# Two transformer layers on one core: the second half's route, its scatter, the weight units and the norm moved to other places in the queues

## What is computed

```python
# layer 0: attention by a running sum, then a mixture of experts
kvt = jnp.cumsum(k * v, axis=-2) * denom
vhat = q * kvt
scores = jax.nn.sigmoid(xf @ gate_w.T)
topk_w, topk_idx = jax.lax.top_k(scores, TOP_K)          # 2 of 8 experts
topk_w = topk_w / (topk_w.sum(axis=-1, keepdims=True) + 1e-20)
shared_out = jax.nn.silu(xf @ shared_wg.T) * (xf @ shared_wu.T) @ shared_wd.T
h = jax.nn.silu(jnp.einsum('td,efd->etf', xf, exp_wg)) * jnp.einsum('td,efd->etf', xf, exp_wu)
all_out = jnp.einsum('etf,edf->etd', h, exp_wd)
```

## Time and profile before

| | us |
|---|---|
| median of 3 runs | 780.81 (777.93 to 781.98) |
| profiled execution | 781.96 |
| its span, first to last instruction | 780.1 |
| PE busy in the span | 678.9 (87%) |
| DVE busy | 523.9 (67%) |
| ACT busy | 390.6 (50%) |
| POOL busy | 355.2 (46%) |

### The profile page before, as it was taken

How to read it: one execution, slowest core, us unless ns; L and a number is a source line. 1 busy time by engine, 2 the same in 40 slices (tenths; PEclk the granted TensorE clock), 3 DMA queues, 4 the chain that set the end, 5 groups by cost and what they waited for, 6 DMA issues and landing times.

```text
span 780.1 us, 13300 instructions
## 1 busy us (share of the span) xinstructions
PE 678.9 (87%) x4656; PEld 543.7 (70%) x4656; DVE 523.9 (67%) x1004; ACT 390.6 (50%) x679; POOL 355.2 (46%) x299
## 2 busy tenths in 40 slices
PE   5897898894959879799989989989988998999996
PEld 4675677784848667577667767767866777777774
DVE  6885855884886746567485858486768668467745
ACT  3644423442543644274575455385448276447263
POOL 1416276376576226145163527164616353416353
PEclk9999899897998999999999999999999999999999
DMA  8427735766885274512003303002402000201100
GB/s 313 130 94 223 267 121 179 224 202 221 294 277 181 77 279 116 179 25 58 2 2 108 82 2 82 2 1 69 121 2 65 19 1 28 62 23 44 39 2 28
DMA packets 66804, 82.76 MB, mean 106 GB/s; under 512 B 7090, under 2 KB 50354, under 8 KB 66738
## 3 DMA queue, kind: packets, MB, share of 16 engines
q1 hardware_dynamic: 63156, 73.39, 29.7%
q0 software_dynamic: 3072, 8.39, 3.3%
q10 hardware_dynamic: 512, 0.13, 0.1%
HBM read 40.34 MB, written 28.84 MB: 89 GB/s over the span
## 4 chain that ended last, share of the span: by engine, by line
PE 37%; ACT 9%; DVE 9%; issue 5%; DMA 2%; POOL 2%; ACTq 1%; POOLq 0%; DVEq 0%
PE acc L632 4%; PE acc L634 3%; PE acc L633 3%; PE pv L632 2%; PE pm L632 2%; PE pm L634 2%; PE pm L633 2%; PE pv L634 2%; PE pv L633 2%; PE ring L955 2%; PE ring L985 2%; DVE hf L2067 2%; DVE mx L2151 2%; ACT act L1428 1%; PE ring L957 1%
## 5 line engine op out<-in xcount | busy, mean ns | idle before, releaser
L1531 POOL TENSOR_TENSOR hl<-hf,hh 128x512 fp32r<-128x512 f32 (+1 forms) x76 | 99.3, 1307 | 231.5 <-ACT hh L1235 231.4
L1235 ACT ACTIVATE hh<-hf 128x512 fp32r<-128x512 f32 (+1 forms) x76 | 47.7, 629 | 85.5 <-DVE hf L2067 69.8
L632 PE MATMUL acc<-hh,wh 128*128 128x512 f32 (+1 forms) x168 | 70.6, 420 | 7.6 <-POOL hl L1531 7.6
L2067 DVE TENSOR_TENSOR hf<-hf,pv 128x512 f32<-128x512 f32 x64 | 43.6, 682 | 39.7 <-PE pv L634 38.6
L2151 DVE TENSOR_REDUCE mx<-ring 128x2 f32<-128x512 f32 (+1 forms) x96 | 61.7, 684 | 11.5 <-PE ring L957 11.3
L633 PE MATMUL acc<-hh,wl 128*128 128x512 f32 (+1 forms) x168 | 66.3, 395 | 0.0
L634 PE MATMUL acc<-hl,wh 128*128 128x512 f32 (+1 forms) x168 | 66.3, 395 | 0.0
L1410 ACT ACTIVATE hf<-pm 128x512 f32<-128x512 f32 x56 | 33.3, 595 | 58.6 <-PE pm L634 55.5
L1672 POOL TENSOR_TENSOR pl<-act,ph 128x512 f16<-128x512 f32 x32 | 41.7, 1303 | 39.9 <-ACT ph L1433 37.0
L632 PE MATMUL pv<-xh,wh 128*128 128x512 f32 x128 | 54.0, 422 | 1.5 <-DVE hf L2067 1.5
L632 PE MATMUL pm<-xh,wh 128*128 128x512 f32 x112 | 48.9, 437 | 2.9 <-issue 2.9
(11 more groups left out here) (289 smaller groups left out, 2117.6 us busy)
## 6 DMA issues: line engine op xcount, KB each, us to landing
w4s<-w4hl SPq DMA_DIRECT2D x16, 512.0 KB, 3.8
ws<-qs SPq DMA_DIRECT2D x12, 512.0 KB, 5.1
qT<-qp SPq DMA_DIRECT2D x96, 64.0 KB, 2.6
kT<-kp SPq DMA_DIRECT2D x96, 64.0 KB, 2.7
xs<-yg SPq DMA_DIRECT2D x2, 2944.0 KB, 12.5
late<-xs SPq DMA_DIRECT2D x22, 256.0 KB, 3.1
ys<-act SPq DMA_DIRECT2D x22, 256.0 KB, 3.4
stage<-w SPq DMA_DIRECT2D x8, 608.0 KB, 4.5
```

What stands on the lines that cost most here:

```text
L632: pe.matmul(o, w_hi, x_hi, start=first, stop=False, skip_group_check=True)
L1235: a.activation(h_parts(n)[0][0:rows, :], hf[0:rows, n % 2, :], ACT.Copy).then_inc(s_hh, 1)
L1531: return pool.tensor_tensor(dst, src, hi.bitcast(F32), ALU.subtract)
L2067: v.tensor_tensor(hf[:, n % 2, :], hf[:, n % 2, :], pv[:, :], ALU.mult).then_inc(s_h, 1)
```

## The change

Tables: `W4_AT` gives every unit from 4 on an odd slot, one every second slot from 3 to 41. The logits and counts of both halves use the banks `pm` and `pv`.

First stage: `turn_logits(1)` and `scores_of(1)` move into group 3. On DVE `residual(1)` goes between `choose(0, 0)` and `choose(0, 1)`; `offsets(0)` and `positions(0)` go behind the first gated tile of group 2, `owners(0)` behind the second; `choose(1, 0)` goes ahead of `rows_lo(0)` and `choose(1, 1)` ahead of `residual(3)`. On POOL `split_h(11)` goes ahead of unit 2.

Expert stage: `shares(1)`, `offsets(1)`, `positions(1)` and `owners(1)` are in slots 0, 1, 2 and 3. The scatter of the second half is dealt out two tiles ahead of each of the units 4 to 7, where three, three and two tiles stood behind units 7, 8 and 9. Gathers 0 to 3 follow units 15 and 16, gathers 4 to 6 go between units 19 and 22; their rows are weighed in slots 30 to 33. The norm's steps come one slot sooner. The eight small loads are spread over slots 6 to 13. `latents(0)` goes ahead of `turn_gated(44)`.

Second stage: the last pair's rows go to `xn`, so its `expert_rows` waits for no store; `latents_std(0)` goes between the last two `expert_rows`; ACT no longer waits for the stores (SP and POOL do, where they need it). In group 0 only `rows_back(7)` is left.

Tables, buffers and SP's queue:

```diff
...
-W4_AT = dict(zip((0, 2, 4, 6, 8, 10, 13, 16, 18, 20, 22, 24, 26, 28, 30, 32, 34, 36, 38, 41), range(4, 2 * NQ)))
+W4_AT = {3 + 2 * i: 4 + i for i in range(2 * NQ - 4)}
...
-            return (pm, acc[:, 0, :])[h]
+            return pm
...
-            return (pv, acc[:, 0, N_EXP * TT:])[h]
+            return pv
...
-            if c < 4:
+            if c < 7:
...
-                        ex[:, 1, :].rearrange("p (b d) -> p b d", d=D), xn[:, 0:2, :])[c]
+                        ex[:, 1, :].rearrange("p (b d) -> p b d", d=D), xn[:, 0:2, :])[c % 4]
+            if c == 7:
+                return apart(act)
...
+        def rows_from(pp):
+            if pp == HALVES * PAIRS - 1:
+                return xn[:, 2:2 + pair_tiles(pp), :]
+            b = 2 * (pp % 2)
+            return rows_out[:, b:b + pair_tiles(pp), :]
...
-                b = 2 * (pp % 2)
-                sp.dma_start(pair_rows(ys_d[pp // PAIRS], pp), rows_out[:, b:b + pair_tiles(pp), :]).then_inc(
-                    s_yd[pp % 2], 16)
+                sp.dma_start(pair_rows(ys_d[pp // PAIRS], pp), rows_from(pp)).then_inc(s_yd[pp % 2], 16)
...
-                if q == 6:
-                    small_in()
+                if 6 <= q < 14:
+                    small_in(q - 6)
...
+            for done in s_yd:
+                sp.wait_ge(done, 16 * PAIRS)
```

TensorE's queue (and at its end `gate1` and `up1` of the second stage):

```diff
...
-                if h:
-                    pe.wait_ge(s_res, G)
...
+                if q == 2:
+                    pe.wait_ge(s_rt, ROUTE_STEPS + 25)
...
-                if g == 1:
-                    turn_logits(0)
+                if g % HG == 1:
+                    turn_logits(g // HG)
...
+                if q == HALVES * TILES - 1:
+                    for i in range(2):
+                        pe.wait_ge(s_wlo[i], len(lo_of[i]))
+                    normed(G)
+                    latents(0)
...
-                if q == 0:
-                    turn_logits(1)
-                if q == 5:
+                if q == 1:
...
-                if q == TILES + 12:
+                if q == TILES + 11:
...
-                if q == TILES + 14:
+                if q == TILES + 13:
...
-                if q == TILES + 16:
+                if q == TILES + 15:
...
-            for i in range(2):
-                pe.wait_ge(s_wlo[i], len(lo_of[i]))
-            normed(G)
-            latents(0)
...
-                        pe.wait_ge(s_yo, HALVES * PAIRS)
+                        pe.wait_ge(s_yo, HALVES * PAIRS - 1)
...
+                    if g == 0 and t == 0:
+                        pe.wait_ge(s_yo, HALVES * PAIRS)
```

ACT's queue:

```diff
...
-                if pp >= 2:
+                if 2 <= pp < HALVES * PAIRS - 1:
...
-                a.activation(rows_out[:, 2 * (pp % 2):2 * (pp % 2) + n, :], bank, ACT.Copy).then_inc(s_yo, 1)
+                a.activation(rows_from(pp), bank, ACT.Copy).then_inc(s_yo, 1)
...
+                if g == G - 1:
+                    scores_of(1)
...
-                if q == 0:
-                    scores_of(1)
...
-                if q == TILES + 15:
+                if q == TILES + 14:
...
-                if q == TILES + 17:
+                if q == TILES + 16:
...
-                if q == TILES + 20:
+                if q == TILES + 19:
...
-            expert_rows(HALVES * PAIRS - 2)
-            expert_rows(HALVES * PAIRS - 1)
-            for done in s_yd:
-                a.wait_ge(done, 16 * PAIRS)
...
+            expert_rows(HALVES * PAIRS - 2)
+            latents_std(0)
+            expert_rows(HALVES * PAIRS - 1)
...
-                    latents_std(b0)
```

POOL's queue:

```diff
...
-                if c in (0, 4):
+                if c in (0, 7):
...
             split_h(9, ST_M[0])
             w4_parts(1)
             split_h(10, ST_M[1])
+            split_h(11, ST_M[2])
             w4_parts(2)
-            split_h(11, ST_M[2])
             w4_parts(3)
             for k in range(4, 8):
+                rows_out_to(1, 2 * k - 8, 2 * k - 7)
                 w4_parts(k)
-            rows_out_to(1, 0, 1, 2)
-            w4_parts(8)
-            rows_out_to(1, 3, 4, 5)
-            w4_parts(9)
-            rows_out_to(1, 6, 7)
-            for k in range(10, 17):
+            for k in range(8, 16):
                 w4_parts(k)
             rows_back(0)
             rows_back(1)
+            w4_parts(16)
+            rows_back(2)
+            rows_back(3)
             w4_parts(17)
-            rows_back(2)
+            weights(13)
             w4_parts(18)
-            rows_back(3)
-            weights(13)
-            for k in range(19, 2 * NQ):
+            w4_parts(19)
+            for k in range(20, 23):
+                rows_back(k - 16)
                 w4_parts(k)
+            w4_parts(23)
 
             pool.wait_ge(s_res, G)
             pool.wait_ge(s_ey, HALVES * TILES)
...
-                more = range(4 * g + 4, 4 * g + 8) if g < G - 1 else ()
+                more = (((), (), (7,), ()) if g == 0 else
+                        [(4 * g + 4 + t,) for t in range(4)] if g < G - 1 else ((),) * 4)
...
-                    for c in more[t:t + 1]:
+                    for c in more[t]:
```

DVE's queue (`bias_latents`, `latent_stats` and `latent_spread` are moved up unchanged):

```diff
...
-                if g == 2:
-                    offsets(0)
-                    positions(0)
-                    owners(0)
-                if g == 3:
-                    codes(2)
...
+                        residual(1)
...
+                    if g == 2 and t == 0:
+                        offsets(0)
+                        positions(0)
...
+                        owners(0)
...
-                    if g == 3 and t == 1:
+                    if g == 3 and t == 0:
+                        codes(2)
+                    if g == 3 and t == 2:
...
-                if g < G - 1:
+                if g in (0, 2):
...
+            def bias_latents(nb):
...
+            def latent_stats(nb):
...
+            def latent_spread(nb):
...
+            choose(1, 0)
...
+            choose(1, 1)
...
+                if q == HALVES * TILES - 1:
+                    bias_latents(0)
...
+                if q == 0:
+                    shares(1)
...
-                    choose(1, 0)
+                    offsets(1)
...
-                    choose(1, 1)
+                    positions(1)
...
-                    shares(1)
-                if q == 5:
-                    offsets(1)
-                if q == 6:
-                    positions(1)
-                if q == 7:
...
-                if q - TILES in (7, 8, 10, 11):
-                    weigh_rows((7, 8, 10, 11).index(q - TILES))
+                if 7 <= q - TILES < 11:
+                    weigh_rows(q - TILES - 7)
...
-                if q == TILES + 13:
+                if q == TILES + 12:
...
-                if q == TILES + 15:
+                if q == TILES + 14:
...
+                if q == TILES + 16:
+                    ln_inverse(G, 0, 1)
...
-                    ln_inverse(G, 0, 1)
+                    ln_inverse(G, 2, 3)
...
-                    ln_inverse(G, 2, 3)
-                if q == TILES + 19:
...
-                if q == TILES + 21:
+                if q == TILES + 20:
...
+            latent_stats(0)
...
+            latent_spread(0)
...
-            def bias_latents(nb):
...
-                    bias_latents(0)
-                    latent_stats(0)
-                    latent_spread(0)
...
```

More of the change, by code:

```diff
@@ L506, in clear, with small_in @@
                 sp.dma_start(rows, yg[:, 0, :].unsqueeze(1).to_broadcast([P, TILES, D])).then_inc(s_fill[h], 16)
-            def small_in():
-                sp.dma_start(bc[:, :], biasc.partition_broadcast(P)).then_inc(s_bc, 16)
-                for t, src in ((bv[:, :], biasv.partition_broadcast(P)), (gb[:, :], cols), (bout[:, :], bo), (spreadf[:, :], spread_c), (ident[:, :], identb_c.bitcast(BF16)),
-                               (maskq[:, :], mask_c[0].bitcast(BF16)), (maskk[:, :], mask_c[1].bitcast(BF16))):
-                    sp.dma_start(t, src).then_inc(s_const, 16)
+            def small_in(i):
+                t, src = ((bc[:, :], biasc.partition_broadcast(P)), (bv[:, :], biasv.partition_broadcast(P)),
+                          (gb[:, :], cols), (bout[:, :], bo), (spreadf[:, :], spread_c),
+                          (ident[:, :], identb_c.bitcast(BF16)), (maskq[:, :], mask_c[0].bitcast(BF16)),
+                          (maskk[:, :], mask_c[1].bitcast(BF16)))[i]
+                sp.dma_start(t, src).then_inc(s_const if i else s_bc, 16)
             tokens_in(0)
@@ L2009, in _ @@
                         codes(1)
[L2010 removed]
+                    if g == 3 and t == 0:
+                        codes(2)
+                    if g == 3 and t == 2:
                         codes(3)
[L2012 removed]
+                if g in (0, 2):
                     residual(g)
[L2015 to L2067 removed]
+            seg = (slice(0, D_Q), slice(D_QR, D_QR + D_KV))
             def bias_latents(nb):
@@ L2087, in latent_spread, with gated1 @@
                     v.bn_aggr(mv[:, i, :], bst[:, i, :]).then_inc(s_bn, 1)
+            choose(1, 0)
```

(54 more changed lines are left out.)

36 lines of the change are left out of this document (removed).

## The result

The kernel after took 769.5 us, median of four executions (768.63 to 770.56), beside 781.35 for the kernel before on the same chip. The ratio is 0.9862 (95% interval 0.9832 to 0.9892), 11 us or 1.4% less time. The forecast of 756.5 us, 24 us less, had the sign and a little over twice the size. The profiled execution took 769.19 us, its span 767.4.

The account below looks back on a forecast made before the run. Bound: TensorE (87% of the span), with some 38 us lost in expert slots to waits on other engines. Terms 6.9 + 2.5 + 5 + 0 + 5 + 5 = 24.4 off 781.96, less 1.15 to the median: 756.5 us; own range 750 to 764, wider 746 to 770.

Parts of the forecast that it names:

- Ahead of the experts and slots 0 to 5: First stage and early expert slots: slot 0 loses 1 us; slot 5 comes 1.3 us sooner in all.
- Slots 5 to 18: Expert stage: scatter starts at 142.9, unit 7 ends at 173.3, slot 18 comes at 183.6; 6.9 us gained (0 to 10).
- Slot 25: Expert stage: ACT's 3.5 us wait for attention weights shrinks to about 1; 2.5 us gained (0 to 3.5).
- Slots 30 to 34: Expert stage: gathers start in slot 27, not 30, fourth tile there near slot 33; 5 us gained (2 to 7.5).
- Slots 34 to 45: Expert stage: norm's mean, variance and split come one slot sooner at the same prices; 0 us (-1 to 1).
- End of the experts: After slot 45: no wait for stores, first GELU 8.1 us later instead of 11.9; 5 us gained (3 to 6).
- The last gather: Second stage: tile 7's gather goes ahead of the 2 MB load, TensorE's 3.4 us stop goes; 5 us (2 to 5.5).
- The rivals: Scatter's wait only moves, 763.4 (0.20); gathers late again, 761.5 (0.08); descriptors starved, 769 (0.05); POOL never catches up, 792 (0.03).
- descriptors are starved: Rival: DVE stretches all 16 scatter issues to 1.78 us, POOL's chain 12.6 us longer; 769 us; chance 0.05.

Follow-up runs that it names:

- p4: Kernel after with the second half's scatter back in groups of three, three and two tiles behind units 7, 8 and 9; ratio 0.9949.
- p13: Kernel after with the second half's scatter dealt one tile to a unit (units 4 to 11) instead of two; ratio 0.9850.
- p14: Kernel after with the edits of p12 and p13 together; 758.74 us, ratio 0.9711.
- p9: Kernel after with only the norm's steps moved back one slot, to where they were before; ratio 0.9831.
- p12: Kernel after with norm, turning and adding of tiles 2, 3 in old slots, `weights(13)` behind unit 22, POOL held for DVE's third and fourth gathered-tile multiplies; 760.56 us.

## Why the prediction was wrong in size

- **Ahead of the experts and slots 0 to 5**: the marks agree, but a single trace does not settle terms this small. Slot 0 came 1.5 us later (1 expected), slot 5 2.0 us sooner (1.3); in the same kernel taken again it was 0.1 us later and 1.1 sooner, and in the thirteen traces here that have the kernel after's order up to there (all but p4, p13 and p14) slot 5 lies between 146.4 and 150.1.
- **Slots 5 to 18**: right, and by the mechanism named. The scatter began at 143.95, its four steps took 7.3 to 8.5 us (7.6 expected), unit 7 was through at 175.2 (173.3), SP issued the codes at 175.26, and ACT had waited 7.55 us for them when it went on at 179.27. Slot 16 came at 180.29 (179.0 expected), slot 18 at 184.25 (183.6). 6.3 us for 6.9.
- **Slot 25**: right. ACT's wait was 0.49 us instead of the 3.50 of the earlier trace rows.
- **Slots 30 to 34**: 4.2 us from slot 26 to 34 for 5. "They start in slot 27" was wrong by one: the stores had not landed by then, and the gathers start when the last one is in, at 210, in slot 28.
- **Slots 34 to 45**: this step failed. I put it at 0 (-1 to 1); it lost 10.9. Both halves of the loss were in sight. "One slot sooner but at the same prices" priced each step and not what stands ready when TensorE reaches it: p9 and p12 give 3.6 and 1.8 us for that. And a DVE step locked behind POOL was priced where I had seen it (the 3.14 us of the earlier trace rows, the 3.96 of the earlier trace rows), but I did not lay POOL's new order beside DVE's: behind gather 3 it has units 17 and 18 with `weights(13)` between them, five instructions and 6.7 us by the durations in the trace, and this run had begun 0.8 us before DVE took up the third tile's rows. No rival had this. Its price was to be had from rows of before: a multiply of a unit takes 1.17 us, and there were four of them and a larger one.
- **End of the experts**: 4.3 us between slot 45 and the GELU (11.87 to 7.61) for 5; undone it cost 5.1.
- **The last gather**: 6.5 us from the GELU to the end for 5; undone it cost 6.0.
- **The rivals**: none happened. 769 was the time of "descriptors are starved", but the 16 scatter issues had medians of 0.98 and 1.23 us, not 1.78, and unit 7 came 2 us late, not 12.6: same number, wrong mechanism. That 769.5 lies within the stated 746 to 770 is therefore luck: the upper end came from that rival.

The length of POOL's run, too, stood in a row of the prediction. Its 3.96 us were read as a wait for "a whole instruction", "the trace agrees". DVE's step ran from 120.51 to 124.47, and POOL's timeline of the kernel before has three instructions in a row there, not one:

```profile
120.63 1.31 POOL L1531 TENSOR_TENSOR hl<-hf,hh 128x512 fp32r<-128x512 f32 x1
121.88 1.17 POOL L1561 TENSOR_TENSOR w4hl<-code,scl_h 128x512 fp32r<-128x512 f16 x1
123.00 1.18 POOL L1562 TENSOR_TENSOR w4hl<-code,ws 128x512 fp32r<-128x512 f16 x1
```

The six terms of the trace, 6.3 + 2.5 + 4.2 - 10.9 + 4.3 + 6.5, are the 12.8 us measured but for rounding; with the loss of slots 34 to 45 taken out again, p12 reached 20.1 us (0.0258 of 780) of the 24.4 forecast.

## What to carry to other kernels

Where GpSimd works through a backlog, lay its list beside VectorE's by time: in these traces the next VectorE step in SBUF alone stood until the backlog was through (3.9 to 6.0 us behind four or five instructions). So break long runs up, or let GpSimd wait where VectorE is ready. A step moved one slot sooner on an in-order engine is free only if its input is there by then; read the wait in front of it, not its duration. When a change speeds up one stage, every part of the sum that stays at "0" deserves a look at what it now meets.

## What was not expected of the hardware

- The lock lasts until the end of GpSimd's whole run, not of one instruction: 5.88, 5.95 and 5.91 us behind five instructions, 3.94 and 3.89 behind four, 0.35 behind none; with one unit at a time (p13) seven `mag` steps took 2.61 to 2.93 us, one unit's two multiplies. By the Trainium skill (SBUF — State Buffer, section on SBUF's two separate sides), where the VectorE step is of a form that needs the ports shared with GpSimd (two SBUF inputs, for one), whichever of the two starts first has them for a whole instruction and the other fully blocks. The trace agrees on the block, but GpSimd went from one instruction to the next four times and VectorE did not get its turn. Why, no run here shows. An indirect DMA that GpSimd issues seems to belong to the run: the multiply of the earlier trace rows (0.34 us elsewhere) began at 226.61, 0.70 us ahead of GpSimd's next multiply and while GpSimd was issuing a gather (226.35, 0.95 us), and stood 3.14 us all the same, until both multiplies behind the gather were through at 229.59.
- In the kernel after it is one-sided. Views by tile of the kernel after (duration ns min/median/max): GpSimd's multiplies stay at 1.2 us, with a longest of 1.46, VectorE's `mag` goes from 0.41 to 3.0, and VectorE's subtractions that read a PSUM bank (`ring`, `acc`) are never longer, though by the two timelines nine of the 44 below fell into a GpSimd multiply:

```profile
L1568 POOL TENSOR_TENSOR w4hl<-code,scl_h x16: 1147/1159/1177, 112.6 to 235.7; 128x512 fp32r<-128x512 f16 x16
```

```profile
L1942 DVE TENSOR_SCALAR mag<-ws x24: 407/415/3025, 95.6 to 265.0; 128x512 uint16<-128x512 uint16 x24
...
L1714 DVE TENSOR_TENSOR htl<-ring,hth x22: 406/410/421, 138.4 to 269.3; 88x256 fp32r<-88x256 f32 x22
L1714 DVE TENSOR_TENSOR htl<-acc,hth x22: 406/410/421, 141.6 to 271.5; 88x256 fp32r<-88x256 f32 x22
```

It is no rule, though. In the kernel before, one multiply of GpSimd took 2.23 us. It began inside a VectorE subtraction with two SBUF inputs; POOL's timeline, and DVE's under it:

```profile
218.08 2.23 POOL L1561 TENSOR_TENSOR w4hl<-code,scl_h 128x512 fp32r<-128x512 f16 x1 [5.51 <-DVE code L1948]
```

```profile
217.92 1.08 DVE L1706 TENSOR_TENSOR al<-xc,ah 128x896 fp32r<-128x896 f32 x1
```

GpSimd waited there for one VectorE step; VectorE waited elsewhere for runs of five.
